# Two attention cores of a four-layer kernel: PE's order from a list schedule, maxima ahead by one group, first loads over two queues

## What is computed

```
scores = einsum('bhqd,bhkd->bhqk', q, k) / sqrt(8)
scores = where(causal, -inf, scores)            # first layer only
attn   = softmax(scores, axis=-1)
out    = einsum('bhqk,bhkd->bhqd', attn, v)
```

## Time and profile before

| | us |
|---|---|
| median of three runs | 4007.14 |
| the profiled execution | 4003.27 |
| its span, from first to last instruction | 4001.5 |
| PE busy | 3295.9 (82%) |
| DVE busy | 2709.7 (68%) |
| ACT busy | 1827.7 (46%) |
| `core0`, from its memsets to its last instruction | 256 to 790 |
| `core1` | 1532 to 2284 |

### The profile page before, as it was taken

One profiled execution on the slowest core, in us unless ns is written; L12 is line 12 of the kernel. 1 busy time (PEld: TensorE's weight loads), 2 busy tenths in 40 slices (PEclk: granted clock), 3 DMA queues, 4 the chain that ended last, 5 costly groups with the idle time before them and its releaser, 6 DMA issues. The chain is left out here.

```text
span 4001.5 us, 60331 instructions
## 1 busy us (share of the span) xinstructions
PE 3295.9 (82%) x19635; PEld 2001.5 (50%) x19635; DVE 2709.7 (68%) x7212; ACT 1827.7 (46%) x2668; POOL 1012.0 (25%) x1089
## 2 busy tenths in 40 slices
PE   4559999977576967999999869789777996997898
PEld 2422333344355852222222258668656784886687
DVE  8888888576876458999999564464566455544453
ACT  1225666665122531677777725323222333553454
POOL 3442330021334631000000036427401660000000
PEclk8869999998787985999999969889877997998899
DMA  1042331000021122000000031221201112000100
GB/s 48 1 140 75 112 115 38 2 1 1 22 91 42 48 74 87 18 18 19 26 19 11 22 147 47 75 89 52 75 1 70 45 47 99 0 0 1 53 0 21
DMA packets 88138, 185.24 MB, mean 46 GB/s; under 512 B 24560, under 2 KB 43056, under 8 KB 84784
## 3 DMA queue, kind: packets, MB, share of 16 engines
q1 hardware_dynamic: 60704, 116.03, 8.7%
q0 software_dynamic: 26576, 64.79, 5.4%
q10 hardware_dynamic: 576, 0.79, 0.1%
HBM read 119.92 MB, written 60.82 MB: 45 GB/s over the span
## 5 line engine op out<-in xcount | busy, mean ns | idle before, releaser
L2127 ACT ACTIVATE core_pr<-core_two 128x1024 f32<-128x1024 f32 (+3 forms) x896 | 794.4, 933 | 442.2 <-PE core_two L2089 441.3
L2153 DVE TENSOR_REDUCE core_mx<-core_one 128x1 f32<-128x512 f32 x1280 | 800.9, 682 | 23.1 <-PE core_one L2073 19.6
L2073 PE MATMUL core_one<-arena,core_q_sb 64*128 64x512 bf16 (+3 forms) x1792 | 548.4, 380 | 107.1 <-DMA core_q_sb<-core_q_sb 44.7
L2073 PEld LDWEIGHTS core_one<-arena,core_q_sb 64*128 64x128 bf16 x1792 | 140.6, 94 | 690.7 <-DVE core_mx L2153 525.8
L2100 PE MATMUL core_ps_o<-core_pr,core_vals 128*32 128x512 f32 (+3 forms) x3584 | 438.9, 562 | 1.6 <-ACT core_oT L2131 0.5
L2089 PE MATMUL core_two<-core_q_sb,arena 64*128 64x512 bf16 (+3 forms) x1792 | 362.5, 362 | 6.4 <-ACT core_pr L2127 5.4
L2150 DVE CUSTOM_DVE_ANT_0 core_junk<-core_one,behind 128x128 bf16<-128x128 f32 (+3 forms) x512 | 230.3, 486 | 58.4 <-PE core_one L2073 53.0
L2021 POOL COPY core_vals<-arena 128x288 f32<-128x288 f32 x32 | 14.5, 455 | 982.6 <-PE core_ps_o L2100 982.5
L341 POOL DMA_INDIRECT expert_out<-arena,moe_first_dest_index x142 | 139.6, 983 | 98.1 <-ACT arena L514 84.7
L341 POOL DMA_INDIRECT expert_out<-arena,moe_second_dest_index x142 | 139.9, 985 | 96.8 <-ACT arena L514 82.8
L451 PE MATMUL moe_second_bank<-arena 128*128 x1136 | 152.0, 277 | 5.7 <-ACT arena L514 5.3
(11 more groups left out here) (538 smaller groups left out, 7431.1 us busy)
## 6 DMA issues: line engine op xcount, KB each, us to landing
arena<-expert_out SPq DMA_DIRECT2D x64, 256.0 KB, 3.0
core_q_sb<-q_parts SPq DMA_DIRECT2D x384, 32.0 KB
arena<-k_parts SPq DMA_DIRECT2D x360, 32.0 KB
expert_rows<-arena SPq DMA_DIRECT2D x16, 512.0 KB, 11.8
core_w_raw<-in_m_up POOLq DMA_DIRECT2D x25, 256.0 KB, 4.3
m_hi<-core_w_hi POOLq DMA_DIRECT2D x25, 256.0 KB, 2.8
m_lo<-core_w_lo POOLq DMA_DIRECT2D x25, 256.0 KB, 3.4
q_parts<-qkv_parts SPq DMA_DIRECT2D x16, 384.0 KB, 2.6
```

The source lines that it names most:

```text
L2073: pe.matmul(one[bank][:, 0:width], q_sb[rows, hq, pair, qt * P:(qt + 1) * P], k_sb[rows, hq, pair, kc * CW:kc * CW + width], start=True, s ...
L2127: a.activation(pr[:, k % 2, hp, :, off:CW], two[hp][:, :, off:CW], ACT.Exp, scale=HD ** -0.5).then_inc(s_exp, 1)
L2153: v.tensor_reduce(mx[:, h * TPB + qt, kc:kc + 1], one[bank][:, 0:width], AX.X, ALU.max).then_inc(s_read, 1)
```

## The change

A function `order` takes the place of `plan`, `banked` and `over_groups`. It builds one list of all events of a stage: at each step it looks at what could be issued next (a first, a turn, a second, a weigh, an out), with estimated costs for PE, ACT and DVE, and takes the one whose engine has the least work ahead. The costs are constants in the code. Its core:

```diff
+        todo = []
+        for n in range(N):
+            late = firsts[n + 1][:4] if n + 1 < N else []
+            early = firsts[n][4:] if n else firsts[n]
+            todo += [*early, ("rows", n, 0, 0), *late[:2], ("turn", n, 0, 0), *late[2:], ("split", n, 0, 0)]
...
+            if second < 2 * N * N2:
+                n, k, i = second // (2 * N2), second // 2 % N2, second % 2
+                if ("known", n) in done and second // 2 - weigh < 2:
+                    options.append((max(wide_free(), done["known", n]), at["act"], "second", ("second", n, k, i)))
+            if weigh < N * N2 and not (moves and weigh % N2 in ends) and ("second", *divmod(weigh, N2), 1) in done:
...
+                options.append((ready, at["act"] - WEIGH_LEAD, "weigh", ("weigh", n, k, 0)))
...
+            now = max(at["pe"], min(o[0] for o in options))
+            ready, _, what, e = min((o for o in options if o[0] <= now), key=lambda o: o[1])
...
+            if what == "first":
+                seen = issue(ready, width * 5 // 24 + 30) + NOTE
+                done[e] = dve(seen, width * 25 // 24 + 80) + NOTE
...
+            elif what == "second":
+                seen = issue(ready, w * 5 // 12 + (107 if steps[k][3] else 0) + 40) + NOTE
+                done[e] = act(seen, w * 5 // 3 + 80) + NOTE
...
+            elif what == "weigh":
+                done["weighed", weigh] = issue(ready, span[k] * 5 // 3 + 140) + NOTE
```

A pair of seconds goes into whichever of the two double banks is next; which side comes first alternates with the instruction before it:

```diff
+            def turns(side, later):
+                if side is not None:
+                    return 1 - side, side
+                begin = tiles(*later[1:3])[later[3]][0] if later and later[0] == "first" else 0
+                return begin, 1 - begin
...
+                    both = turns(None if mask else last, later)
+                    for side in both:
```

The order stays fixed in the program, and the waits are the same in kind; they are on counts worked out from the list, without the counts that semaphores were set to at the start. The wait of the first second of a group:

```diff
                     if k == 0 and i == 0:
                         pe.wait_ge(s_mld, (n + 1) * 32)
```

The loads: ACT fetches the keys of groups 0 and 1, SP all other rows; the three rows are cleared by a copy only from group 4 on, since the memset has cleared them for the first four. The memsets write pairs of bf16 as one fp32:

```diff
+                fetch_rows(sp, 0, n)
+                if n >= 2:
+                    fetch_rows(sp, 1, n)
+                if n >= GROUPS:
+                    for y in range(2):
+                        at = y * HALF + QK_ROWS
+                        sp.dma_start(q_sb[at:at + 3, hq], q_sb[at + 3:at + 6, hq]).then_inc(s_loaded[hq], 16)
...
-                p.memset(q_sb[:, hq], 0.0).then_inc(s_zero, 1)
+                p.memset(q_sb[:, hq].bitcast(F32), 0.0).then_inc(s_zero, 1)
...
+            for n in range(2):
+                a.wait_ge(s_ones, n + 1)
+                fetch_rows(a, 1, n)
...
-                v.memset(k_sb[:, hq], 1.0).then_inc(s_ones, 1)
+                v.memset(k_sb[:, hq].bitcast(F32), TWO_ONES).then_inc(s_ones, 1)
```

More of the change, by code:

```diff
@@ L1852, in core_stage @@
     ps_o = st.ps("ps_o")
[L1854 to L1861 removed]
+    units = list(itertools.product(range(PAIRED), range(TPB)))
     steps = []
@@ L1928, in over_groups @@
-    def over_groups(eng, emit):
-        whole, head, tail = range(N1), range(HEAD), range(HEAD, N1)
-        def group(b, hq, firsts, before, second=True, more=1):
-            for what, k, ahead, bank in banked(plan(firsts, second, more), before):
-                emit(what, k, *after(b, hq, ahead), bank)
-        group(0, 0, [(0, whole), (1, head)], [], False, 0)
-        steady = [("first", HEAD - 1, 1), ("out", 1, -1)]
-        for b in range(BATCH - 1):
-            for hq in range(GROUPS):
-                group(b, hq, [(1, tail), (2, head)], steady)
-        for hq in range(GROUPS):
-            left = GROUPS - 1 - hq
-            group(BATCH - 1, hq, [(1, tail), (2, head)][:min(left, 2)], steady if left else [("maxima", 0, 0), ("out", 1, -1)], True, min(left, 1))
@@ new lines, in core_stage @@
+    events = order()
+    LOADS = 2 * 2 * len(PAIRS)
+    nth, count, ring, wide = {}, {}, [], []
+    for e in events:
+        nth[e] = count.get(e[0], 0)
+        count[e[0]] = nth[e] + 1
+        if e[0] in ("first", "turn", "out"):
+            ring.append(e)
+        elif e[0] == "second":
+            wide.append(e)
+    bank = {e: i % len(one) for i, e in enumerate(ring)}
+    earlier = {e: ring[i - len(one)] if i >= len(one) else None for i, e in enumerate(ring)}
+    spot = {e: i for i, e in enumerate(wide)}
@@ new lines, in turns @@
+            def turns(side, later):
[3 more added lines that the diff above has]
+                return begin, 1 - begin
+            work = [e for e in events if e[0] in ("first", "turn", "second", "weigh", "out")]
+            last = None
+            for e, later in itertools.zip_longest(work, work[1:]):
+                what, n, k, i = e
+                hq = n % GROUPS
+                if what == "first":
+                    pair, qt = units[k]
+                    side, width, kc = tiles(n, k)[i]
+                    rows, _ = lane(side)
+                    if k == i == 0:
+                        pe.wait_ge(s_loaded[hq], fetched(n))
+                    wait_bank(e)
+                    pe.matmul(one[bank[e]][:, 0:width], q_sb[rows, hq, pair, qt * P:(qt + 1) * P],
@@ L2074, in emit @@
                               k_sb[rows, hq, pair, kc * CW:kc * CW + width], start=True, stop=True).then_inc(s_first, 1)
-                elif what == "maxima":
+                    last = side
+                elif what == "turn":
+                    wait_bank(e)
                     pe.wait_ge(s_row, n + 1)
-                    pe.matmul(one[bank][0:GH * TPB, 0:P], mrow[:], g.ident[:], start=True, stop=True).then_inc(s_first, 2)
-                elif what in ("second0", "second1"):
+                    pe.matmul(one[bank[e]][0:GH * TPB, 0:P], mrow[:], g.ident[:], start=True, stop=True).then_inc(s_rowT, 1)
+                    last = None
+                elif what == "second":
```

389 lines of the change are left out of this document (205 added, 184 removed).

## The result

| | before | changed |
|---|---|---|
| median, us | 4007.11 | 4122.86 (4116.77 to 4126.85) |
| ratio | | 1.0285, 95% interval 1.0265 to 1.0306 |
| profiled execution, its span | 4003.27, 4001.5 | 4124.89, 4123.1 |
| `core0`, first memset to last instruction | 534.0 | 624.5 |
| `core1` | 751.6 | 786.4 |

The span grew by 121.6 us: 90.5 in `core0`, 34.8 in `core1`, and the stages around them changed by 3.7 the other way (a stage is taken to the start of its last instruction, 0.3 us before its end). The forecast was 4075: the side was right, the size was not, and the difference lies in `core0`.

The account below looks back on a forecast made before the run. It took PE to bound `core0` and DVE `core1`; +30.5 us in `core0`, +41.7 in `core1` and -3.6 for first loads made +69 on 4003.3, 4072, stated as 4075. Range 3965 to 4115, the forecast's own 4035 to 4105.

Parts of the forecast that it names:

- The sum: Both stages: `core0` 15 x 32.7 - 461.0 + 1 = +30.5, `core1` +41.7, first loads -3.6, together +69 us.
- The gap and its length: Before each `core0` group's first seconds: PE arrives 7.5 us after the turn, stands 3.5; period 31.4 us before the clock.
- the chain of the maxima: Turn, two firsts, split, store, two loads, PE's wait: now on the path between groups, 7.2 us in `core0`.
- the gain by the sides: Alternating array halves in `core0` lets a first and a second overlap: 0.1 us at some six places, 0.6 a group.
- The clock in `core0`: Granted clock falls at group starts in 55 of 100 groups, at 2.3 us each: period 31.4 + 1.3 = 32.7.
- maxima come later: Rival: weight traffic delays the maxima 2 us more a `core0` group, clock falling each time; 4120 us, chance 0.08.
- 0.7 for exp and bank waits: Added to `core0`'s period for waits in the dense part: 0.7 us a group.
- the right sum from two wrong terms: `core1` period: 44.0 us (32.4 plus a stretch of 11.6 between groups) plus 2.5 for the clock, 46.5.
- the dense part: The 16 steps before the gap in each `core1` group: 2.0 us a step, 32.4 us in all.
- the -1.8 us a stage of the loads: Start of each stage: without clearing copies and with smaller memsets first loads land sooner, -1.8 us, bounds -0.5 and -4.
- Ends: From last store to stage end: `core0` 32.5 us, so +1; `core1` 39.5, so -3.8.
- What would show it: Signs: periods 32 to 33.5 and 46 to 47, low clock 5 to 8 us in `core1`, in half of `core0`'s groups.

Follow-up runs that it names:

- fixed_order_less_ahead: The kernel before with a quarter of the next group's first scores run ahead of the maxima in place of half; ratio 1.0344 to the kernel before.

## Why the prediction was right or wrong

**The sum.** First store to last: `core0` 549.0 us, predicted 15 x 32.7 = 490.5; `core1` 690.5, predicted 697.5. `core0` alone is 58.5 us over the sum.

**The gap and its length: the number was right in `core0`.** 31.4 us a group without the clock; measured 31.75. From the turn to the masked matmul it is 7.46 us in the group without weights (777.18 to 784.64), where I had 7.5. But the text called the chain of the maxima the path, and without the weights PE did not stop for them: it had the firsts in front of the wait to do, at DVE's pace, and the chain of 7.2 just fits behind them. It was also lucky by 0.6: the gain by the sides did not come, and without it the sum gives 32.0.

**The clock in `core0`: the step that failed first.** I took 55 groups in 100 at 2.3 us, 1.3 on the mean. The size of 2.3 was right for a group without weights (2.35), but the clock falls in every group, and with the weights it costs 3.4 to 4.0. The only row that I had of a fall in `core0` was at a start of a group with a stop for the maxima; that the clock would stay up in 45 of 100 had no row behind it.

**The weights' traffic: left out of the sum.** It costs 1.5 to 2.1 us a group by itself. The rival "maxima come later" described what happened in `core0`: 1.7 us later to the masked matmul (6.26 against 4.59), the clock falling each time, 4120. I gave it 0.08. It was to be read in the trace before: POOL's copy for the next values, and behind it the weights, waits for a group's last weigh [the row 462.50 above]; a store moved from 10 us ahead of it to that very moment runs into it. I checked what SP has queued and not what POOL does at the store's new time.

So a group with weights was to take 32.7 and takes 37.3. Of these 4.6 us, 0.35 are the group without clock and weights (31.75 against 31.4), 1.05 the clock that falls in every group, 1.5 to 2.1 the weights, and the rest, 1.1 to 1.7, the longer low clock beside them. The groups without weights bring the mean down to 36.6.

**The list's own order.** In `core0` 0.8 us a group (31.3 against 30.5, lead kept), which the 0.7 for exp and bank waits covered. In `core1` I took the dense part at 2.0 us a step; measured 1.98 (most steps take 1.96 and 1.99 in turn).

**`core1`: the right sum from two wrong terms.** 46.5 predicted, 46.0 measured. PE and SP around one gap there: the last but one weigh, the firsts that wait for the split, the store, the next seconds.

```profile
2039.37 1.07 PE L2165 MATMUL core_ps_o<-core_pr,core_vals 128*32 128x512 f32 x8
...
2048.13 0.94 PE L2132 MATMUL core_one<-arena,core_q_sb 64*128 64x512 bf16 x3 [1.88 <-DVE core_left L2227]
...
2053.71 1.36 PE L2153 MATMUL core_two<-core_q_sb,arena 64*128 64x512 bf16 x4
```

From the last but one weigh to the next seconds it is 14.3 us here and 12.7 in the group before, 13.5 on the mean, where I had 11.6. Some 1.1 of the difference lie ahead of the store: the bank of the out is free only after its norm, which leaves DVE 0.48 us without work, and the turn holds its bank until the split has read it, which leaves PE 1.88 us without one. The other 0.8 lie behind the store (5.05 and 5.67 us to the seconds, where I had 4.6), and no group of `core1` but the last has a stop for the maxima: there too PE has firsts to do in front of the wait. The clock costs 1.2 and not 2.5; its low stretch ends 3.6 to 4.8 us into the dense part, whose first steps wait for ACT. The errors, +1.9 and -1.3, nearly cancel, and the dense part is about 1 us shorter than I had it.

**Sides and first loads.** The -0.6 us a group of the sides were nothing, and the -1.8 us a stage of the loads some -0.8, inside their bounds.

**Ends.** From the last store to the end 32.0 us in `core0` (predicted 32.5) and 40.5 in `core1` (39.5). Not in the sum: the first store now stands behind two to four firsts more, 1.5 us a stage from the first matmul on.

**What would show it.** ACT's gap of over 6 us (8 to 9 and 12 to 14) and DVE's 0.91 in `core1` came as said, and so did the period of 46.0. The low clock came in every group of `core0` and not in half, and it lasts 10 us in `core1` and not 5 to 8; `core0`'s 32 to 33.5 did not come. And the forecast's own range had a slip: with its bounds of 34 and 47.5 it reaches to 4110 and not 4105.

## What to carry to other kernels

A list schedule that feeds the engine with the least work ahead spends a lead that a fixed pattern keeps: hold the lead as a condition of its own, longer than the path that it hides, and no longer. When an instruction moves, look at what every other queue does at its new time, those included that it never waits for. And where a gap is filled at another engine's pace, as in these two stages, count the low clock in every group and not in some.

## What the runs showed of the hardware

The granted clock fell in gaps in which PE never stopped for long. In the group without weights, whose store is at 745.84, PE's longest stop ahead of the fall was 0.79 us, and it was busy 3.37 of 5.4 us:

```profile
745.80:751.20 5.40, 3.37 (x18) 1.39 (x18) 5.30 (x19) 0.11 (x1) 0.00 (x0) 1.00 0.11 32
751.20:758.00 6.80, 6.80 (x31) 1.54 (x30) 3.94 (x12) 3.86 (x5) 0.00 (x0) 0.50 0.30 82
```

In the groups with weights it fell ahead of their stop for the maxima, after none over 1.0; in the gap in `core1` shown above after one of 1.88. And in `core1` of `fixed_order_less_ahead` it stayed at 1.00 through a stop of 1.0 to 1.6 us between dense work in every group. So the longest stop does not tell these cases apart; ahead of each fall shown, PE was busy only in part.

In `core0` the clock stayed at 1.00 when half-array matmuls of no use were put beside the same firsts, which made the kernel faster by 2.35 us a group. In `core1` one such matmul a first was not enough, and with two it stayed up in some groups only. The Trainium skill ("TensorE: Matmul & The Clock Gate", section "Why this matters for your kernels") names long idle gaps between bursts as what brings the lower clock. By that row alone it would have stayed at 2.4 GHz here; the traces say otherwise.

The weights' DMAs, nine of 256 KB a group issued in threes, put 1.7 us on the 4.6 us from the store of the maxima to the matmul that needs them. And the first loads over two queues brought PE to its first matmul hardly sooner. The Trainium skill ("DMA: Bandwidth & Descriptors", section "Issuing engines are not separate DMA queues") says that DMAs of different engines run on the same 16 DMA engines and interleave. The 1.7 us agree, where POOL's DMAs delay SP's; the first loads' ratio of 0.9995 (0.9985 to 1.0005) does not speak against it.
